# Expert stage: both rows of a pair are added up by the matrix engine alone, without quarter sums on POOL

## Chip, cores and metric

One core of one Trainium2 chip. The metric is the device time of the kernel in microseconds (us), median of several runs. Engines are named as in the profile: PE is TensorE's matmul, PEld its weight load, DVE is VectorE, ACT is ScalarE, POOL is GpSimd, SP is SyncE, whose queue carries the DMAs.

## What is computed

A block of four layers on x of shape (1, 128, 128, 32) in float32; each layer is a token mixer and a channel mixer, both with a residual. The change touches the last channel mixer alone, a mixture of 8 experts with the best 2 per token:

```
router_probs = softmax(x @ router_w + router_b)
top_p, top_i = top_k(router_probs, 2);  top_p = top_p / sum(top_p)
expert_out = einsum('bnd,edc->bnec', x, expert_w) + expert_b
out = einsum('bnk,bnkc->bnc', top_p, take_along_axis(expert_out, top_i[..., None], axis=2))
t = t + out
```

The kernel multiplies all 8 expert outputs of a token by its weights (zero for the 6 that were not chosen) and adds the 8 products up.

## The kernel before

The kernel is written engine by engine: each engine has its own list of instructions in program order, and semaphores hold them together. The eight layer parts follow one another (t0, f0, t1, r1, the scan, r2, t3, f3 in the blocks from L1972 on). The change touches f3, the expert stage, which is the last.

In f3 the 128 x 128 tokens lie as 32 steps s (S = 32) of 128 partitions with G = 4 groups each, so a step has 4 x 32 = 128 output columns (GC) for each of 8 experts: 1024 products a partition. Two steps make a pair j; there are 16 pairs (EPAIRS). The work on a pair goes round four engines:

- PE, expert(s), L1760: the product of the normalised tokens with all expert weights, 4 matmuls of 256 columns into four PSUM banks (L1772, even s; each uses 32 rows of the array) or two banks (L1767, odd s; 64 rows). It waits until the weighing of step s - 2 has read the bank (semaphore e_mul).
- DVE, weigh(s), L1867: one operation over 128 x 1024 that multiplies the products in PSUM by the token's weights and writes WEIGHED in SBUF (L1871).
- POOL, half_sum(s), L1907: adds experts 4 to 7 to experts 0 to 3, 128 x 512, into HALVES (L1909). HALVES has four slots of pairs; a slot holds [expert quarter e = 0..3][step of the pair][128 columns].
- POOL, quarter_sum(j), L1912: for the odd step of the pair alone, adds quarters 2 and 3 to 0 and 1 in place, 128 x 256 (L1914). It follows the odd step's half sum and waits for it (e_half).
- PE, add_up(j), L1775: adds what is left with matmuls against the identity, which sum in PSUM: quarter 0 of both steps (256 columns, L1787), quarters 2 and 3 of the even step alone (128 columns each, L1789), quarter 1 of both steps (256 columns, L1790).
- DVE, add_pair(j), L1874: adds x from SBUF to the sum in PSUM and writes x_rows (L1876); SP stores four rows at a time from there.

The order on PE is expert(2j), expert(2j + 1), add_up(j - 2) (SUM_LAG = 2); on DVE weigh(2j), weigh(2j + 1), add_pair(j - 2). DVE also does the routing of the second half of the tokens between the weighings of pairs 1 to 5 (L1881 to L1888; L1833, L1834 and L1853 are among it). The half sum of the last step, 31, and the quarter sum of the last pair run on DVE (L1893 to L1895), with a semaphore of their own (e_last).

A float32 matmul is two weight loads and two matmul instructions in the trace, so that one call of pe.matmul shows as "x2".

Of the kernel before, what the change touches and what calls it, by code (L numbers as in the profile page):

```python
# [28 lines left out]
GC = G * C  # L29
# [9 lines left out]
E3 = 8  # L39
# [75 lines left out]
def build(nc, x_d, par_d, row_d, mask_d, w1_d, w2_d, w2l_d, out_d):  # L115
    with ExitStack() as ctx:
        def sb(name, shape, dt=F32):
            return ctx.enter_context(nc.sbuf_tensor(name, shape, dt))

        def sem(name):  # L120
            return ctx.enter_context(nc.semaphore(name))
# [3 lines left out]
        XC = sb("x_cols", [N, NC])  # L125
# [13 lines left out]
        ident = sb("ident", [N, N])  # L139
# [11 lines left out]
        eps = sb("eps", [N, 4])  # L151
# [8 lines left out]
        last = sb("last", [C, G, C])  # L160
# [5 lines left out]
        def bank(b, cols=BANK, n=1):  # L166
            return PSUM[:, b * BANK:b * BANK + (n - 1) * BANK + cols]
# [42 lines left out]
        def stage(name, kinds, own="", src=None, dst=None, scratch=None, eps=0, e2=0.0):  # L210
            L = Stage(name, src, dst, scratch, eps, e2)
            for kind in kinds.split():
                if kind not in shared:
                    shared[kind] = [0, {}]
                    for word in families[kind].split():
                        shared[kind][1][word.split(":")[0]] = sem(f"{kind}_{word.split(':')[0]}")
                before, sems = shared[kind]
                shared[kind][0] += 1
                for word in families[kind].split():
                    key, n = word.split(":")  # L220
                    L.s[key], L.at[key] = sems[key], before * int(n)
            for key in own.split():
                L.s[key], L.at[key] = sem(f"{name}_{key}"), 0
            return L
# [15 lines left out]
        def wait_all(eng, levels):  # L240
            for s, v in levels:
                eng.wait_ge(s, v)
# [9 lines left out]
        v2 = stage("V2", "turn_x")  # L252
        r2 = stage("R2", "scale last turn rec check", "g_ps g_y0 g_y1 g_edge_ps g_edge g_turned y_ps done", src=XC, eps=1, e2=0.0)
        t3 = stage("L3", "norm last weights ones tri", src=XC, scratch=XR, eps=0, e2=EPS)
        f3 = stage("F3", "norm last ones turn", "c_dve w_dve w_pe rank hot rt_ps top diff sg e_ps e_mul e_half e_last e_quart e_sum done", src=XC, eps=1, e2=0.0)


        x_done = lambda L: [(L.s["done"], L.at["done"] + S // 4)]
# [203 lines left out]
        def turn_z_pe(pe, L, b):  # L462
            wait_z(pe, L, b)
            if "one" in L.s:
                pe.wait_ge(L.s["one"], L.at["one"] + b + 1)
            if b >= 2:
                pe.wait_ge(L.s["zt"], L.at["zt"] + b - 1)
            for k in range(4):
                m = pe.transpose(bank(b % 2)[:, k * N:(k + 1) * N], block_of(Z)(4 * b + k), ident[:, :])  # L469
            m.then_inc(L.s["zt_ps"], 1)  # L470
# [414 lines left out]
        top = sb("top", [N, 6, K0])  # L885
# [808 lines left out]
        rank = sb("rank", [N, E3], BF16)  # L1694
# [6 lines left out]
        EPAIRS = S // 2  # L1701
        SUM_LAG = 2
        WEIGHED = GATE[:, :].rearrange("p (k f) -> p k f", k=4)
        HALVES = Z[:, :].rearrange("p (j e k f) -> p j e k f", j=4, e=E3 // 2, k=2)
# [30 lines left out]
        def f3_pe(pe):  # L1735
            L = f3
            pe.wait_ge(L.s["w_dve"], L.at["w_dve"] + 2)

            def route(b):

                pe.wait_ge(L.s["zt"], L.at["zt"] + b + 1)
                for s in range(4 * b, 4 * b + 4):
                    m = pe.matmul(bank(6 + s // 16)[:, s % 16 * G * E3:(s % 16 + 1) * G * E3], ZT[:, s, :], wr[:, :, :],
                                  start=True, stop=True)
                return m

            for b in range(S // 4):
                turn_z_pe(pe, L, b)
                if b == 3:
                    wait_all(pe, L.early_banks_free)  # L1750
                    for a in range(b - 1):
                        route(a)
                if b >= 3:
                    m = route(b - 1)
                if b == 4:
                    m.then_inc(L.s["rt_ps"], 1)
            wait_all(pe, L.banks_free)
            route(7).then_inc(L.s["rt_ps"], 1)

            def expert(s):  # L1760
                if s >= 2:
                    pe.wait_ge(L.s["e_mul"], L.at["e_mul"] + s - 1)
                if s % 2:
                    for q in range(2):
                        for h in range(2):
                            rows = slice(h * HALF_ROWS, (h + 1) * HALF_ROWS)
                            m = pe.matmul(bank(4 + h)[:, q * E3 * C:(q + 1) * E3 * C], ZT[rows, s, :], we[rows, q, :],  # L1767
                                          start=True, stop=True)
                else:
                    for g in range(G):  # L1770
                        rows = slice(g * C, (g + 1) * C)
                        m = pe.matmul(bank(g, E3 * C), ZT[rows, s, :], we[rows, g % 2, :], start=True, stop=True)  # L1772
                m.then_inc(L.s["e_ps"], 1)

            def add_up(j):  # L1775

                pe.wait_ge(L.s["e_half"], L.at["e_half"] + min(2 * j + 2, S - 1))
                if j < EPAIRS - 1:
                    pe.wait_ge(L.s["e_quart"], L.at["e_quart"] + j + 1)
                else:  # L1780
                    pe.wait_ge(L.s["e_last"], L.at["e_last"] + 2)
                if j == 0:
                    pe.wait_ge(L.s["top"], L.at["top"] + F3_LOGITS_READ)
                if j >= 2:
                    pe.wait_ge(L.s["done"], L.at["done"] + j - 1)
                o = bank(6 + j % 2, 2 * GC)
                pe.matmul(o, ident[:, :], HALVES[:, j % 4, 0, :, :], start=True, stop=False)  # L1787
                for e in (2, 3):
                    pe.matmul(o[:, 0:GC], ident[:, :], HALVES[:, j % 4, e, 0, :], start=False, stop=False)  # L1789
                pe.matmul(o, ident[:, :], HALVES[:, j % 4, 1, :, :], start=False, stop=True).then_inc(L.s["e_sum"], 1)  # L1790

            for j in range(EPAIRS):
                expert(2 * j)
                expert(2 * j + 1)
                if j >= SUM_LAG:
                    add_up(j - SUM_LAG)
            for j in range(EPAIRS - SUM_LAG, EPAIRS):
                add_up(j)
# [10 lines left out]
        def f3_dve(dve):  # L1809
            L = f3  # L1810
# [80 lines left out]
                    add_pair(j - SUM_LAG)  # L1891
            dve.wait_ge(L.s["e_mul"], L.at["e_mul"] + S)
            half_sum(dve, S - 1, "e_last")  # L1893
            dve.wait_ge(L.s["e_last"], L.at["e_last"] + 1)
            quarter_sum(dve, EPAIRS - 1, "e_last")  # L1895
            for j in range(EPAIRS - SUM_LAG, EPAIRS):
                add_pair(j)

# [8 lines left out]
        def half_sum(eng, s, done="e_half"):  # L1907
            halves = WEIGHED[:, s % 4, :].rearrange("p (a e f) -> p a e f", a=2, f=GC)
            eng.tensor_tensor(HALVES[:, s // 2 % 4, :, s % 2, :], halves[:, 0], halves[:, 1], ALU.add)\  # L1909
                .then_inc(f3.s[done], 1)  # L1910

        def quarter_sum(eng, j, done="e_quart"):  # L1912
            halves = HALVES[:, j % 4, :, 1, :]
            eng.tensor_tensor(halves[:, 0:2], halves[:, 0:2], halves[:, 2:4], ALU.add).then_inc(f3.s[done], 1)  # L1914

        def f3_pool(pool):
            L = f3
            for a in range(2):
                half = slice(a * N // 2, (a + 1) * N // 2)
                pool.wait_ge(L.s["sg"], L.at["sg"] + 2 * a + 1)  # L1920
                pool.tensor_tensor(RT[5][:, half], RT[1][:, half], W1S[:, half].unsqueeze(2).to_broadcast([N, N // 2, E3]),
                                   ALU.mult).then_inc(L.s["hot"], 1)
            for s in range(S - 1):
                pool.wait_ge(L.s["e_mul"], L.at["e_mul"] + s + 1)
                if s >= 8:
                    pool.wait_ge(L.s["e_sum"], L.at["e_sum"] + s // 2 - 3)
                half_sum(pool, s)
                if s % 2:
                    pool.wait_ge(L.s["e_half"], L.at["e_half"] + s + 1)
                    quarter_sum(pool, s // 2)  # L1930


        for L, b, col in ((t0, 2, 0), (t1, 0, 0), (t3, 1, 0), (f3, 4, 0), (r1, 5, 0), (r2, 5, GC)):
# [165 lines left out]
```

## Time and profile before

| | |
|---|---|
| runs | 531.54, 531.96, 533.02 us (median 531.96) |
| profiled execution | 531.37 us, span 529.5 us |
| busy | PE 425.5 us (80%), DVE 366.6 (69%), ACT 234.5 (44%), POOL 227.2 (43%) |
| mean granted TensorE clock | 0.900 of full speed (2.4 GHz) |
| expert stage | from about 461 us to the end |

The span goes from the first to the last instruction; the run's time has some 2 us more around it. A share of busy time is a mean over all layers, most of which the change does not touch; for the change it is the expert stage that has to be read. PE's rows are pipelined: the row of a matmul includes the way through the array, so that rows of one engine overlap, and the start of one row to the start of the next tells what an instruction costs in a sequence. Where several instructions of a line follow one another, the timeline shows them as one row with their count.

### The profile page before, as it was taken

What the parts mean: (1) busy time and instruction counts of PE and PEld (TensorE: products, weight loads), DVE (VectorE), ACT (ScalarE), POOL (GpSimd) and SP (SyncE); (2) the same over time, 40 slices, a digit from 0 to 9 for tenths busy, and PEclk for the clock granted to TensorE, in tenths of its full rate; (3) what the DMA queues carried; (4) which work ended last, traced back from release to release, by engine and by line L of the source; (5) the groups of instructions that cost most, each with busy time, mean ns of one, the idle gap of its engine ahead of it and who ended that gap; (6) DMA issues with size and microseconds to landing.
All of it is one profiled execution on the core that took longest, in us unless ns stands there. A gap on an engine that the chain in (4) does not pass through costs nothing.

```text
span 529.5 us, 8983 instructions
## 1 busy us (share of the span) xinstructions
PE 425.5 (80%) x3226; PEld 321.7 (61%) x3226; DVE 366.6 (69%) x1191; ACT 234.5 (44%) x577; POOL 227.2 (43%) x294
## 2 busy tenths in 40 slices
PE   2788866987698866998599968698589877869995
PEld 2455853566344853797399945598355866736664
DVE  4887688748798388637634467301979389998885
ACT  1397654621577456677400038476369553300000
POOL 2499178001477078000000035000349369268994
PEclk9999999778799899999779979799579978569999
DMA  9400000000000000000000000000000000001223
GB/s 170 84 2 1 1 1 0 1 3 0 1 2 1 0 2 1 1 2 1 2 0 1 1 3 0 1 2 1 0 2 2 1 0 1 2 0 20 41 45 56
DMA packets 34671, 6.05 MB, mean 11 GB/s; under 512 B 33713, under 2 KB 34369, under 8 KB 34626
## 3 DMA queue, kind: packets, MB, share of 16 engines
q1 hardware_dynamic: 34626, 5.46, 5.9%
q8 instruction: 27, 0.44, 0.3%
q14 instruction: 18, 0.15, 0.1%
HBM read 3.36 MB, written 2.10 MB: 10 GB/s over the span
## 4 chain that ended last, share of the span: by engine, by line
PE 48%; DVE 37%; ACT 5%; POOL 5%; issue 3%; DMA 1%; SPq 1%; DVEq 0%; POOLq 0%
PE psum L1594 7%; DVE ab L750 6%; PE psum L1167 5%; DVE moments L334 5%; PE psum L1166 5%; DVE ab L734 5%; PE psum L469 3%; PE psum L624 3%; PE psum L1767 3%; POOL z L394 2%; PE psum L594 2%; PE psum L635 2%; PE psum L1787 2%; POOL gate L812 2%; PE psum L1772 2%
## 5 line engine op out<-in xcount | busy, mean ns | idle before, releaser
L594 PE MATMUL psum<-wp_L,z_t 64*128 64x320 f32 x384 | 66.1, 473 | 3.4 <-ACT z_t L372 2.1
L334 DVE BATCH_NORM_STATS2 moments<-x_cols 128x6 f32<-128x64 f32 x448 | 61.8, 214 | 3.1 <-ACT x_cols L873 1.8
L469 PE MATMUL psum<-ident,z 128*128 128x128 f32 x224 | 43.4, 332 | 22.3 <-POOL z L394 19.4
L469 PEld LDWEIGHTS psum<-ident,z 128*128 128x128 f32 x224 | 31.2, 170 | 45.7 <-POOL z L394 33.1
L372 ACT ACTIVATE z_t<-psum 128x512 f32<-128x512 f32 x56 | 40.0, 720 | 31.1 <-PE psum L469 30.9
L594 PEld LDWEIGHTS psum<-wp_L,z_t 64*128 64x128 f32 x384 | 33.3, 192 | 31.0 <-issue 27.6
L389 POOL MEMSET z<- 128x16 f32 x32 | 4.0, 126 | 112.1 <-DVE z L320 111.7
L1302 ACT ACTIVATE ab<-psum,mv 128x128 f32<-128x128 f32 x108 | 39.7, 368 | 16.2 <-PE psum L1167 5.9
L1167 PE MATMUL psum<-ab,R_vt 128*128 128x128 f32 x216 | 45.7, 294 | 0.0
L812 POOL TENSOR_TENSOR gate<-gate,stats 128x512 f32<-128x512 f32 x24 | 25.2, 1050 | 44.2 <-DVE stats L775 43.9
L1166 PE MATMUL psum<-z_t,wbnt 128*128 128x128 f32 x216 | 43.3, 283 | 0.8 <-DVE wbnt L1364 0.8
L635 PE MATMUL psum<-wo_L,z_t 64*128 64x128 f32 x384 | 29.8, 297 | 15.7 <-DVE x_cols L783 8.5
L1594 PE MATMUL psum<-ab,toep 128*128 128x128 f32 x324 | 39.0, 284 | 4.1 <-POOL ab L1575 3.1
L1594 PEld LDWEIGHTS psum<-ab,toep 128*128 128x128 f32 x324 | 38.7, 199 | 4.5 <-issue 4.5
L1909 POOL TENSOR_TENSOR z<-gate 128x512 f32<-128x512 f32 x31 | 39.9, 1304 | 1.4 <-DVE gate L1871 1.4
L1871 DVE TENSOR_TENSOR gate<-psum,ab 128x1024 f32<-128x1024 f32 x32 | 37.9, 1220 | 3.1 <-PE psum L1772 3.0
L362 ACT ACTIVATE stats<-moments,eps 128x16 f32<-128x16 f32 x56 | 17.3, 309 | 48.6 <-DVE moments L334 48.5
L750 DVE TENSOR_TENSOR ab<-psum,sig 128x256 f32<-128x256 f32 x64 | 34.6, 608 | 6.0 <-ACT sig L681 6.0
L635 PEld LDWEIGHTS psum<-wo_L,z_t 64*128 64x128 f32 x384 | 25.4, 199 | 20.7 <-ACT z_t L702 10.7
L681 ACT ACTIVATE sig<-psum 128x256 f32<-128x256 f32 x96 | 36.8, 384 | 0.0
L718 POOL TENSOR_TENSOR x_rows<-gate,bo_L 128x512 f32<-128x512 f32 x24 | 30.6, 1276 | 12.4 <-ACT gate L677 12.3
L1166 PEld LDWEIGHTS psum<-z_t,wbnt 128*128 128x128 f32 x216 | 34.0, 198 | 1.3 <-DVE wbnt L1364 1.3
(271 smaller groups left out, 905.3 us busy)
## 6 DMA issues: line engine op xcount, KB each, us to landing
x_cols<-in_x_dram SPq DMA_DIRECT2D x16, 128.0 KB, 2.8
out_dram<-x_rows SPq DMA_DIRECT2D x32, 64.0 KB, 1.9
par<-in_par_dram SPq DMA_DIRECT2D x1, 644.5 KB
w<-in_w_dram SPq DMA_DIRECT2D x4, 64.0 KB, 2.3
w<-in_w_dram SPq DMA_DIRECT2D x1, 256.0 KB, 2.5
mask<-in_mask_dram SPq DMA_DIRECT2D x1, 64.0 KB, 2.8
row<-in_row_dram SPq DMA_DIRECT2D x1, 3.3 KB
w_bias<-in_w_dram SPq DMA_DIRECT2D x1, 8.0 KB, 1.8
```

Source lines behind the costliest of these rows:

```text
L334: m = dve.bn_stats(moments[:, q, k:k + 2, :].rearrange("p k m -> p (k m)"), X4[:, SQ * q + s, g:g + 2, :].rearrange("p g c -> p c g"))
L372: act.activation(dst, bank(q % 2).rearrange("p (s n) -> p s n", s=4), ACT.Copy).then_inc(L.s["zt"], 1)
L469: m = pe.transpose(bank(b % 2)[:, k * N:(k + 1) * N], block_of(Z)(4 * b + k), ident[:, :])
L594: m = pe.matmul(bank(slot_bank(s) + h, 2 * 5 * C), ZT[rows, s, :], wp[l][rows, :, :], start=True, stop=True)
L635: m = pe.matmul(o_bank(b)[:, :, 2 * h:2 * h + 2, k, :], ZT[rows, 4 * b + k, :], wo[l][rows, :, rows].rearrange("p w (g c) -> p w g c", g=2 ...
L750: dve.tensor_tensor(to_ab(s).rearrange("p (h g) w -> p h g w", h=2), slot(s)[:, :, :, 2 * C:4 * C], sig, ALU.mult).then_inc(L.s["lin"], 1)
L1166: return (pe.matmul(o, W["wbnt"][:, :], chunks(ZTIME, off, h), start=True, stop=False), lambda: pe.matmul(o, W["vt"][:, :], chunks(Y, off, ...
L1167: lambda: pe.matmul(o, W["vt"][:, :], chunks(Y, off, h), start=False, stop=True))
L1302: act.activation(chunks(Y, first + k + 1, h), bank(2 * h + (before + k) % 2, NS), ACT.Sigmoid, bias=bias).then_inc(L.s[f"step_y{h}"], 1)
L1594: m = pe.matmul(bank(2 + h, ROWS_S * NB), toep[:, b, :, :], scan_rows(SCN[:, :, b:b + NB], off, h), start=(b == 0), stop=(b == 2))
L1871: dve.tensor_tensor(WEIGHED[:, s % 4, :].rearrange("p (e g c) -> p e g c", e=E3, g=G), f3_out(s), wts[:, s].unsqueeze(3).to_broadcast([N, ...
L1909: eng.tensor_tensor(HALVES[:, s // 2 % 4, :, s % 2, :], halves[:, 0], halves[:, 1], ALU.add)\
```

## The change

The quarter sums are gone on POOL and on DVE, with their semaphore e_quart. add_up(j) takes all four quarters of both steps: four matmuls of 256 columns against the identity, in one accumulation. It waits for the half sums (e_half), and in the last pair for one event of e_last instead of two.

```diff
@@ add_up(j), PE
                 pe.wait_ge(L.s["e_half"], L.at["e_half"] + min(2 * j + 2, S - 1))
-                if j < EPAIRS - 1:
-                    pe.wait_ge(L.s["e_quart"], L.at["e_quart"] + j + 1)
-                else:
-                    pe.wait_ge(L.s["e_last"], L.at["e_last"] + 2)
+                if j == EPAIRS - 1:
+                    pe.wait_ge(L.s["e_last"], L.at["e_last"] + 1)
...
                 o = bank(6 + j % 2, 2 * GC)
-                pe.matmul(o, ident[:, :], HALVES[:, j % 4, 0, :, :], start=True, stop=False)
-                for e in (2, 3):
-                    pe.matmul(o[:, 0:GC], ident[:, :], HALVES[:, j % 4, e, 0, :], start=False, stop=False)
-                pe.matmul(o, ident[:, :], HALVES[:, j % 4, 1, :, :], start=False, stop=True).then_inc(L.s["e_sum"], 1)
+                for e in range(E3 // 2):
+                    m = pe.matmul(o, ident[:, :], HALVES[:, j % 4, e, :, :], start=(e == 0), stop=(e == E3 // 2 - 1))
+                m.then_inc(L.s["e_sum"], 1)
@@ f3_dve, after the last weighing
             half_sum(dve, S - 1, "e_last")
-            dve.wait_ge(L.s["e_last"], L.at["e_last"] + 1)
-            quarter_sum(dve, EPAIRS - 1, "e_last")
@@ quarter_sum
-        def quarter_sum(eng, j, done="e_quart"):
-            halves = HALVES[:, j % 4, :, 1, :]
-            eng.tensor_tensor(halves[:, 0:2], halves[:, 0:2], halves[:, 2:4], ALU.add).then_inc(f3.s[done], 1)
@@ f3_pool
                 half_sum(pool, s)
-                if s % 2:
-                    pool.wait_ge(L.s["e_half"], L.at["e_half"] + s + 1)
-                    quarter_sum(pool, s // 2)
```

The end of PE's list shows the last expert products and the add_ups of pairs 13 to 15. A row's count is of calls of pe.matmul; the semaphores that it waits for stand behind it (names begin with the stage, F3). Before:

```order
L1772 MATMUL psum<-we,z_t 128x256 [waits F3_e_mul]
L1772 MATMUL psum<-we,z_t 128x256 x3
L1767 MATMUL psum<-we,z_t 128x256 [waits F3_e_mul]
L1767 MATMUL psum<-we,z_t 128x256 x3
L1787 MATMUL psum<-z,ident 128x256 [waits F3_done,F3_e_quart,F3_e_half]
L1789 MATMUL psum<-z,ident 128x128 x2
L1790 MATMUL psum<-z,ident 128x256
```

With the change:

```order
L1772 MATMUL psum<-we,z_t 128x256 [waits F3_e_mul]
L1772 MATMUL psum<-we,z_t 128x256 x3
L1767 MATMUL psum<-we,z_t 128x256 [waits F3_e_mul]
L1767 MATMUL psum<-we,z_t 128x256 x3
L1786 MATMUL psum<-z,ident 128x256 [waits F3_done,F3_e_half]
L1786 MATMUL psum<-z,ident 128x256 x3
```

The place of add_up in the list is the same; it is four matmuls as before, two of them twice as wide, and one wait fewer at its head.

The end of DVE's list, from the last weighing on. Before:

```order
L1871 TENSOR_TENSOR gate<-psum,ab 128x1024 x2
L1876 TENSOR_TENSOR x_rows<-x_cols,psum 128x2x4x32
L1909 TENSOR_TENSOR z<-gate 128x4x128
L1914 TENSOR_TENSOR z<-z 128x2x128
L1876 TENSOR_TENSOR x_rows<-x_cols,psum 128x2x4x32 x2
```

With the change:

```order
L1868 TENSOR_TENSOR gate<-psum,ab 128x1024 x2
L1873 TENSOR_TENSOR x_rows<-x_cols,psum 128x2x4x32
L1904 TENSOR_TENSOR z<-gate 128x4x128
L1873 TENSOR_TENSOR x_rows<-x_cols,psum 128x2x4x32 x2
```

The quarter sum between the last half sum and the last two adds to x is gone (line numbers are smaller by 3 to 5). On POOL the fifteen quarter sums are gone from between the half sums, and the 31 half sums follow one another.

## Rows read from the trace of the kernel before

**Rows 1.** The chain of waits, 450 us to the end, shares by line (longest first).
```profile
by line: PE psum L1767 18.7%; PE psum L1787 12.5%; PE psum L1772 11.3%; PE psum L1789 8.8%; PE psum L1790 8.5%; DVE gate L1871 7.4%; issue 4.0%; DVE ranks L1833 3.4%; DVE ab L1839 2.8%; DVE ranks L1834 2.7%; DVE rmax L1838 2.6%; DVE ab L185
```

**Rows 2.** Busy time by stretch: us, busy us (instructions) by engine, granted clock, DMA.
```profile
487.00:521.00 34.00, 33.97 (x252) 22.37 (x248) 29.99 (x33) 0.00 (x0) 33.14 (x32) 1.00 0.25 40
```

**Rows 3.** Timeline of one pair: start us, us, engine, line, operation, idle before and releaser.
```profile
511.36 0.71 PE L1772 MATMUL psum<-we,z_t 32*128 32x256 f32 x8
...
511.54 2.50 POOL L1909 TENSOR_TENSOR z<-gate 128x512 f32<-128x512 f32 x2
...
512.01 1.13 PE L1767 MATMUL psum<-we,z_t 64*128 64x256 f32 x8
512.14 2.36 DVE L1871 TENSOR_TENSOR gate<-psum,ab 128x1024 f32<-128x1024 f32 x2 [0.25 <-PE psum L1772]
513.07 0.30 PEld L1787 LDWEIGHTS psum<-z,ident 128*128 128x128 f32 x2 [0.33 <-POOL z L1909]
513.07 0.70 PE L1787 MATMUL psum<-z,ident 128*128 128x256 f32 x2
...
513.61 0.61 PE L1789 MATMUL psum<-z,ident 128*128 128x128 f32 x4
...
514.05 0.60 PE L1790 MATMUL psum<-z,ident 128*128 128x256 f32 x2
514.12 0.73 POOL L1914 TENSOR_TENSOR z<-z 128x256 f32<-128x256 f32 x1
...
514.58 0.71 PE L1772 MATMUL psum<-we,z_t 32*128 32x256 f32 x8
```

**Rows 4.** Line L1790 from 487 to 521 us: duration in ns, min/median/max.
```profile
L1790 PE MATMUL psum<-z,ident x22: 379/380/382, 488.2 to 520.7; 128*128 128x256 f32 x22
```

**Rows 5.** Timeline of PE around the first add_up, 470 to 484 us.
```profile
474.22 2.08 PE L1767 MATMUL psum<-we,z_t 64*128 64x256 f32 x8 [1.02 <-DVE gate L1871]
476.23 1.22 PE L1787 MATMUL psum<-z,ident 128*128 128x256 f32 x2
477.24 1.06 PE L1789 MATMUL psum<-z,ident 128*128 128x128 f32 x4
478.10 0.91 PE L1790 MATMUL psum<-z,ident 128*128 128x256 f32 x2
478.93 0.71 PE L1772 MATMUL psum<-we,z_t 32*128 32x256 f32 x8
```

**Rows 6.** Busy time by stretch, where the granted clock rises.
```profile
478.00:479.00 1.00, 1.00 (x8) 0.50 (x7) 0.12 (x1) 0.00 (x0) 0.80 (x1) 0.64 0.00 0
```

**Rows 7.** Timeline from 452 us, routing operations of DVE.
```profile
464.04 0.42 DVE L1834 TENSOR_TENSOR ranks<-ranks,rank 128x512 bf16<-128x512 bf16 x1
...
472.07 0.83 DVE L1834 TENSOR_TENSOR ranks<-ranks,rank 128x512 bf16<-128x512 bf16 x1
...
484.07 0.79 DVE L1853 TENSOR_TENSOR ab<-ab,squares 128x512 f32<-128x512 f32 x1
```

**Rows 8.** Timeline of the end of the stage, from 517.5 us.
```profile
517.79 0.71 PE L1772 MATMUL psum<-we,z_t 32*128 32x256 f32 x8
...
518.06 2.50 POOL L1909 TENSOR_TENSOR z<-gate 128x512 f32<-128x512 f32 x2
...
521.31 1.27 POOL L1909 TENSOR_TENSOR z<-gate 128x512 f32<-128x512 f32 x1
...
521.46 0.67 PE L1787 MATMUL psum<-z,ident 128*128 128x256 f32 x2 [0.37 <-issue]
521.46 1.67 DVE L1909 TENSOR_TENSOR z<-gate 128x512 f32<-128x512 f32 x1
...
523.16 0.42 DVE L1914 TENSOR_TENSOR z<-z 128x256 f32<-128x256 f32 x1
...
523.68 0.67 PE L1787 MATMUL psum<-z,ident 128*128 128x256 f32 x2 [0.68 <-issue]
...
525.27 0.42 DVE L1876 TENSOR_TENSOR x_rows<-x_cols,psum 128x256 f32<-128x256 f32 x1 [1.36 <-PE psum L1790]
```

More of the change, by code:

```diff
@@ L254, in build @@
         t3 = stage("L3", "norm last weights ones tri", src=XC, scratch=XR, eps=0, e2=EPS)
-        f3 = stage("F3", "norm last ones turn", "c_dve w_dve w_pe rank hot rt_ps top diff sg e_ps e_mul e_half e_last e_quart e_sum done", src=XC, eps=1, e2=0.0)
+        f3 = stage("F3", "norm last ones turn", "c_dve w_dve w_pe rank hot rt_ps top diff sg e_ps e_mul e_half e_last e_sum done", src=XC, eps=1, e2=0.0)
         x_done = lambda L: [(L.s["done"], L.at["done"] + S // 4)]
```

## Prediction

> **What bounds the kernel now.** I read the chain of waits first, cut to the last 80 us [rows 1]: nearly all of the change's stage is a chain of matrix engine (PE) lines, the two expert products (L1767, L1772) and the four matmuls of add_up (L1787 to L1790); the weighing on VectorE (L1871) holds 7.4%, and no POOL line is among the large shares. Then the busy time by stretch [rows 2]: from 487 to 521 us PE is busy 33.97 of 34.00 us at a granted clock of 1.00, POOL 33.14, DVE 29.99. Two engines look full, so the timeline of one pair of rows has to tell which sets the pace [rows 3]. PE goes round from one even expert product to the next in 514.58 - 511.36 = 3.22 us, and each of its lines starts where the one before gives way: 0.65 for the even product, 1.06 for the odd one, 0.54 + 0.44 + 0.53 = 1.51 for add_up. POOL needs 3.26 (its halves start at 511.54 [rows 3] and, two pairs on, at 518.06 [rows 8]), so it falls behind by 0.04 a pair. Yet PE does not wait for it: pair 12's quarter sum is there at 514.12 + 0.73 = 514.85 us, and its add_up comes a round after pair 11's, at 513.07 + 3.22 = 516.29 [rows 3]. Only pair 14's, with no expert product ahead of it, finds POOL late: the two half sums before it end at 518.06 + 2.50 = 520.56, its quarter sum some 0.8 later, and the add_up, ready 1.71 + 1.51 after pair 15's product at 521.01, starts at 521.46 [rows 8]. So PE sets the pace, POOL is 1% behind the bound, DVE has 0.44 us a pair to spare (2.36 + 0.42 of 3.22).
>
> The row that could mislead is the weight load's "0.33 idle, POOL z L1909" [rows 3]. The same 0.33 stands before other groups with other releasers, and the half sum that it names had ended long before; I read it as the fixed cost of a group's head, not as a wait for POOL.
>
> **What the change does to PE, pair by pair.** An identity matmul over 128 columns becomes one over 256, twice in each of 16 pairs; each is two instructions in the trace. L1789's four instructions take 514.05 - 513.61 = 0.44 us, 0.11 each [rows 3]. For 256 columns the spacing follows from L1790: two instructions span 0.60 us and the second lasts 0.38 [rows 4], so it starts 0.22 after the first. Four instructions go from 0.11 to 0.22: **+0.44 us a pair**, and the pace becomes 3.22 + 0.44 = 3.66. Bounds: nothing, if the head's 0.33 were room; and 2 x 0.53 - 0.44 = +0.62, if every new matmul cost what a whole L1787 or L1790 takes from its start to the next line's (0.54, 0.53), which has a group's head or a change of line in it. The new ones lie in the middle of a group, as L1787's second instruction does, so I take 0.44.
>
> From pair 3's even product (478.93 us [rows 5]) to pair 15's (517.79 [rows 8]) are 12 rounds in 38.86 us. Twelve at 3.216 would be 38.59; the remaining 0.27 comes from two extra routing operations on DVE in pairs 4 and 5 (the first is the 0.79 of L1853 [rows 7]). At 3.66 DVE's 2.78 + 0.79 = 3.57 fits in a round, so these no longer show. 12 x 0.44 - 0.27 = **+5.0 us**.
>
> **The first add_up** lies in the low clock: its two L1789 matmuls take 478.10 - 477.24 = 0.86 [rows 5], and the granted clock is 0.64 between 478 and 479 us, where it goes from the 1.2 GHz level to the 2.4 GHz level [rows 6]. PE had been busy without a break since 474.22. If the clock rises at the same moment (about 478.7), 1.4 of the 1.72 us that four wide instructions of 0.43 take are spent when it rises, the rest goes at half the price: +0.6 instead of +0.87, or +0.44 if it rose earlier. I take **+0.6**.
>
> **What leaves POOL and DVE.** Fifteen quarter sums leave POOL (0.73 each in the steady part, of which none but the last is on the path). With them POOL's round is 2.50 in 3.66, and its half sums come earlier than now; nothing else waits for it. The cover of this saving is PE: as long as PE needs over 2.50, POOL's gain is worth nothing. Only at the end does it count. The matmuls also lose a wait on the semaphore of the quarter sums; what is queued behind is on PE itself.
>
> **The end**, counted from pair 15's even product (T = 517.79) [rows 8]. Now: add_up of pair 13 at T + 1.71, of 14 at + 3.67 (after POOL's late quarter sum), DVE's half sum of row 31 from 521.46 for 1.67 us (it ends 0.55 after POOL's half sum of row 30, started at 521.31, of usual length 1.27), its quarter sum 0.42, then the last add_up at 523.68 and the last add to x at 525.27, T + 7.48. Changed: add_up of 13 is 1.95 long, so 14 starts at + 3.66 and 15 at + 5.61. By then both half sums are there: POOL's at about + 3.3 without the lag, DVE's from + 4.1 for 0.6 to 1.7. The last add_up takes 525.27 - 523.68 = 1.59 + 0.44, so the last add to x stands at + 7.64: **+0.2 us**. What POOL and DVE save here (some 1.1 us) is what three longer add_ups give back. The stores behind it are the same. Bounds -0.3 and +0.4, for the 0.42 of the quarter sum and its wait either way.
>
> One price stays open at the start. DVE's routing work of row 471 to 473 is on the path, and L1834 takes 0.83 there against 0.42 where POOL is idle [rows 7]. POOL will run the next half sum there instead of the quarter sum. I take 0, between -0.5 (no overlap) and +0.5 (one more such collision).
>
> **Sum:** 5.0 + 0.6 + 0.2 = +5.8 us. The profiled execution had 531.37 us, which makes 537.2; it lies 0.59 below the median of the runs (531.96), on which the same sum gives 537.8. I give 537.5. With the bounds (-0.2 and +0.3 for the first add_up, -0.3 and +0.4 for the end, 0.5 each way for the start, and the runs' own 531.54 to 533.02) the forecast's own range is 535.7 to 539.2.
>
> **Rivals.**
>
> (a) *The pace stays, the new columns fit into the 0.33 us before each group.* For it: those gaps are in the rows as idle time of the weight load. Against it: PE's matmul rows leave 0.03 us of 34 open [rows 2], and starts follow column counts (0.11 for 128, 0.22 for 256). Then only the end changes: add_up of 14 at + 3.22, of 15 at + 4.73, the last add at + 6.3, so -1.1 us: 530.3, inside no change. Chance 0.05.
>
> (b) *Faster: POOL sets the pace.* POOL's round (3.26) is longer than PE's (3.22), and PE's rows stretch by waiting inside it. The quarter sums gone, the next bound is DVE's 2.78: 12 x 0.44 = 5.3 us less, with the 1.1 at the end 525.0. It decides in its favour if PE's true work in a pair, with the 0.44 added, is under 2.78. For it: POOL is busy 33.14 of 34 and named as the releaser of L1787. Against it: the 1.44 us between pair 12's quarter sum and its add_up, and the spacing by columns. Chance 0.03.
> The Trainium skill ("Perfetto Trace Analysis", Identifying the Most-Contended Engine) says that matmul busy time is no good measure of TensorE's headroom, and to take the busy share of the weight loads instead. By that rule PE would be 22.37 / 34 = 66% used here, with 1.1 us of a pair free: this rival's case. I hold the starts of the rows against it.
>
> (c) *Slower than forecast: each new matmul at the upper price.* 0.62 a pair: 12 x 0.62 - 0.27 = 7.2, with 0.8 for the first and 0.4 for the end 8.4 us: 539.8 on the profiled execution, 540.4 on the median. Chance 0.07.
>
> (d) *The clock rises one pair later.* At the low level the odd product takes 2.01 us from start to start (474.22 to 476.23 [rows 5]) against 1.06, so a pair that is still at that level costs some 3.2 us more: 540.7. PE's activity before the rise is the same as now, which speaks against it. Chance 0.05.
>
> **How the numbers follow.** The forecast has 0.80. A difference of 0.3% (1.6 us) is about what a measurement of this kernel tells from none; slower by more are the forecast, (c) and (d): 0.92; within it is (a): 0.05; faster is (b): 0.03. The range of 535.7 to 539.2 is that of the forecast and leaves out the four rivals, 0.20 together.
>
> **What would show it.** In the changed profile: 64 add_up matmuls of 256 columns, 128 instructions; the pair's round at 3.65 to 3.66 us at granted clock 1.00; PE without gaps from about 474 us; POOL idle over 1 us in each round, waiting for DVE's weighing; DVE idle about 0.9 a round, waiting for PE; the last two add_ups starting back to back. A round under 3.4 us would refute the price of a column or the claim that PE is full; a round over 3.8 the spacing in the group; a round of 3.66 with a sum far from +5.8 us would put the error into the first add_up or the end.

## The result and the profile after

The changed kernel took 539.16 us in the median (536.87 to 542.87, 4 runs) beside 532.1 of the kernel before: a ratio of 1.014 (95% interval 1.0102 to 1.0179). The direction was forecast, the size was not: on the median of 531.96 the ratio gives 539.4 us, above the forecast of 537.5 and just above its range. Measured twice more the ratio was 1.0116 (1.0084 to 1.0148) and 1.0103 (1.007 to 1.0136). Over all runs, which come from more than one chip, the medians are 537.99 us (16 runs) and 531.66 (81 runs of the kernel before): **6.3 us** is the better estimate of what the change costs.

The profiled execution of the changed kernel had 540.68 us and a span of 538.7. Its steady part is what the prediction said. One round of a pair (timeline; columns as in [rows 3]):

```profile
519.98 0.71 PE L1772 MATMUL psum<-we,z_t 32*128 32x256 f32 x8
...
521.69 1.99 PE L1786 MATMUL psum<-z,ident 128*128 128x256 f32 x8
522.07 2.50 POOL L1904 TENSOR_TENSOR z<-gate 128x512 f32<-128x512 f32 x2 [1.14 <-DVE gate L1868]
...
523.61 0.71 PE L1772 MATMUL psum<-we,z_t 32*128 32x256 f32 x8
523.72 0.42 DVE L1873 TENSOR_TENSOR x_rows<-x_cols,psum 128x256 f32<-128x256 f32 x1 [0.60 <-PE psum L1786]
```

523.61 - 519.98 = 3.63 us against 3.22 [rows 3]. Add_up now goes from 521.69 to 523.61, 1.92 us instead of 1.51. POOL runs two half sums and then waits 1.14 us a round for the weighing, DVE waits 0.60 for add_up. The busy time by stretch, in the row that answers to [rows 2]:

```profile
487.00:521.00 34.00, 34.00 (x230) 22.61 (x230) 26.84 (x31) 0.00 (x0) 24.51 (x20) 1.00 0.25 40
```

PE is full as before (34.00 of 34), at the same granted clock; POOL has gone from 33.14 to 24.51. In the chain of waits from 450 us on, the line that does all of add_up stands first with 35.3%, where its three parts had 29.8% together [rows 1]:

```profile
by line: PE psum L1786 35.3%; PE psum L1767 17.0%; PE psum L1772 10.7%; DVE gate L1868 4.0%; DVE ranks L1830 3.0%; DVE ranks L1831 3.0%; DVE ab L1836 2.5%; issue 2.4%; DVE moments L334 2.4%; DVE rmax L1835 2.3%; DVE ab L1843 1.6%; DVE squar
```

The end of the stage (timeline, answering to [rows 8]) has no wait for POOL left:

```profile
527.25 0.71 PE L1772 MATMUL psum<-we,z_t 32*128 32x256 f32 x8
...
528.95 5.45 PE L1786 MATMUL psum<-z,ident 128*128 128x256 f32 x24
529.33 1.27 POOL L1904 TENSOR_TENSOR z<-gate 128x512 f32<-128x512 f32 x1 [1.13 <-DVE gate L1868]
530.99 0.42 DVE L1873 TENSOR_TENSOR x_rows<-x_cols,psum 128x256 f32<-128x256 f32 x1 [0.60 <-PE psum L1786]
...
532.71 0.42 DVE L1873 TENSOR_TENSOR x_rows<-x_cols,psum 128x256 f32<-128x256 f32 x1 [0.70 <-PE psum L1786]
534.44 0.42 DVE L1873 TENSOR_TENSOR x_rows<-x_cols,psum 128x256 f32<-128x256 f32 x1 [1.31 <-PE psum L1786]
```

Three add_ups run back to back (528.95, 24 instructions); the adds to x follow at 1.72 us, and the last is 534.44 - 527.25 = 7.19 us behind pair 15's even product, against 7.48.

The opening is where the profile differs from the forecast:

```profile
473.27 4.16 POOL L1904 TENSOR_TENSOR z<-gate 128x512 f32<-128x512 f32 x3
...
476.24 0.72 PE L1772 MATMUL psum<-we,z_t 32*128 32x256 f32 x8
476.34 1.37 DVE L1831 TENSOR_TENSOR ranks<-ranks,rank 128x512 bf16<-128x512 bf16 x1
...
479.02 1.44 PE L1767 MATMUL psum<-we,z_t 64*128 64x256 f32 x8 [2.06 <-DVE gate L1868]
...
480.39 3.33 PE L1786 MATMUL psum<-z,ident 128*128 128x256 f32 x8
...
483.65 0.71 PE L1772 MATMUL psum<-we,z_t 32*128 32x256 f32 x8
```

DVE's second routing operation of pair 1 (L1831, before: L1834) takes 1.37 us instead of 0.83 [rows 7]. PE then stands idle for 2.06 us ahead of the odd product of pair 2, and the first add_up takes 483.65 - 480.39 = 3.26 us, where the steady part needs 1.92. It runs at the 1.2 GHz level almost throughout, as the busy time by stretch shows (columns as in [rows 6]; the clock is the third number from the end):

```profile
480.00:482.00 2.00, 2.00 (x8) 1.34 (x5) 1.97 (x3) 0.00 (x0) 1.54 (x2) 0.50 0.00 0
```

This profile also began the stage late: pair 0's even product is at 466.07 us, against 461.81 before. No instruction ahead of that was changed. The first products of all fourteen profiles of this study, most of changed stages, lie between 459.39 and 466.07, of the kernel before at 461.81 and 463.70, of the changed one at 466.07, 461.76 and 461.94: the layers ahead end earlier or later from execution to execution, and this one drew the latest. That is 4.3 of the 9.2 us between the two profiled spans, and it is no part of the change.

### The profile page after: what moved, and what is told of

Same layout as the page of the kernel before. It is cut to its first block, busy times and chain, and to the rows that moved or that the text cites. A ratio compares the mean times of both kernels' runs of the same rounds, so it can differ in the third digit from the quotient of the medians.

```text
span 538.7 us, 8966 instructions
## 1 busy us (share of the span) xinstructions
PE 435.9 (81%) x3226; PEld 330.7 (61%) x3226; DVE 366.2 (68%) x1190; ACT 234.2 (43%) x577; POOL 216.0 (40%) x279
## 2 busy tenths in 40 slices
DMA packets 34670, 6.04 MB, mean 11 GB/s; under 512 B 33713, under 2 KB 34369, under 8 KB 34626
## 4 chain that ended last, share of the span: by engine, by line
PE 51%; DVE 35%; ACT 5%; POOL 4%; issue 3%; DMA 1%; SPq 1%; DVEq 0%; POOLq 0%
PE psum L1594 7%; DVE ab L750 6%; PE psum L1786 6%; DVE moments L334 5%; PE psum L1167 5%; PE psum L1166 5%; DVE ab L734 5%; PE psum L469 3%; PE psum L624 3%; PE psum L1767 3%; PE psum L635 2%; PE psum L594 2%; POOL z L394 2%; PE psum L1772 2%; ACT z_t L372 2%
```

## The experiments

The stage is cut in three parts below, all start to start: the opening from the even product of pair 0 to that of pair 3, twelve rounds from there to pair 15, the end from there to the last add to x. (Some expectations count the opening from the last routing matmul, which is 0.3 to 0.4 us more.)

| kernel | opening | 12 rounds | end | stage |
|---|---|---|---|---|
| before, two profiles | 17.12, 14.99 | 38.86, 39.76 | 7.48, 7.45 | 63.46, 62.20 |
| changed, three profiles | 17.58, 17.84, 17.58 | 43.60, 43.59, 43.59 | 7.19 | 68.37, 68.62, 68.36 |
| changed, quarter sums left on POOL | 15.41, 15.41 | 43.92, 43.91 | 7.19 | 66.52, 66.51 |
| changed, pair 0's quarter sum left | 15.42 | 44.34 | 7.19 | 66.95 |
| changed, half sum of row 2 held | 15.01, 14.99 | 44.36, 44.36 | 7.19 | 66.56, 66.54 |
| half the change | 14.93 | 41.48 | 6.78 | 63.19 |
| before without quarter sums | 17.04 | 38.81 | 6.04 | 61.89 |
| before, held | 14.59 | 39.96 | 7.47 | 62.02 |
| before, held, two pairs wide | 14.59 | 39.96 | 6.78 | 61.33 |

When PE begins its idle time ahead of the odd product of pair 2, the granted clock is at 1.00 in twelve of these fourteen profiles (early rise). In the first of the kernel before and the second of the changed kernel it is 0.50 there and rises within the first add_up (late rise; 0.64 and 0.65 from 478 to 479 us). These two are compared with one another, the others among themselves.

### The changed kernel once more

No edit.

> The changed kernel once more, to see how its 7.1 us over the kernel before divide. Theory A (columns on PE, and in the layers ahead a granted clock that falls out anew in every execution): the round of a pair is 3.63 us again, the expert stage is 4.9 us longer than before (from the last routing matmul to the last add to x), and whatever is over that lies ahead of the stage, where the times of the runs spread over some 6 us, at mean clocks from 0.886 to 0.900; runs of the kernel before spread likewise when there are more of them. Theory B (the change itself slows the layers ahead): every run of this kernel has its stage begin 2 to 6 us later than the kernel before, and the runs of the kernel before stay within 1.5 us. Median by A 536.5 to 538.5 or what the draw gives, by B 539 again.

Measured: ratio 1.0116 (1.0084 to 1.0148), median 538.26 of 6 runs. The round is 3.63 again. In this profile the stage began at 461.76, as before (461.81), and the clock rose at the same point of the stage, so it can be laid on the first profile of before: 68.62 - 63.46 = 5.2 us longer, +0.7 in the opening, +4.7 in the rounds, -0.3 at the end. The first add_up and the idle time ahead of it (timeline), and the clock by stretch:

```profile
474.71 2.08 PE L1767 MATMUL psum<-we,z_t 64*128 64x256 f32 x8 [1.56 <-DVE gate L1868]
...
476.72 2.95 PE L1786 MATMUL psum<-z,ident 128*128 128x256 f32 x8
...
479.60 0.71 PE L1772 MATMUL psum<-we,z_t 32*128 32x256 f32 x8
```

```profile
476.00:478.00 2.00, 2.00 (x7) 1.17 (x6) 1.93 (x3) 0.00 (x0) 1.22 (x1) 0.50 0.00 0
```

Theory B does not hold: its profile begins no later, and 26 runs of the kernel before on that chip reach from 529.27 to 535.42. But theory A leaves over a microsecond of the 6.3 unexplained.

### Only PE widened: quarter sums stay on POOL

```diff
+        QSCR = sb("qscr", [N, 2, GC])
...
                 half_sum(pool, s)
+                if s % 2:
+                    pool.wait_ge(L.s["e_half"], L.at["e_half"] + s + 1)
+                    halves = HALVES[:, s // 2 % 4, :, 1, :]
+                    pool.tensor_tensor(QSCR[:, :, :], halves[:, 0:2], halves[:, 2:4], ALU.add)
```

Nobody reads QSCR.

> The changed kernel with the fifteen quarter sums left on POOL, written to a buffer that nobody reads, so that PE's four wide matmuls and their waits stay as changed. Theory A: PE's round stays 3.63 us since POOL's 3.26 fits into it; the stage is as long as the changed one to 0.4 us (only the last half sum on POOL could be later). Rival (POOL's freed time is worth something): the stage is longer than the changed one by up to 15 x 0.04 = 0.6 us in the rounds or by 0.7 at the end.

Measured: 1.0068 (1.0038 to 1.0097), median 535.69; measured again 1.0061 (1.0037 to 1.0085), 535.99. One round in the first profile:

```profile
511.45 0.71 PE L1773 MATMUL psum<-we,z_t 32*128 32x256 f32 x8
...
512.48 0.72 POOL L1923 TENSOR_TENSOR qscr<-z 128x256 f32<-128x256 f32 x1
...
515.08 0.71 PE L1773 MATMUL psum<-we,z_t 32*128 32x256 f32 x8
```

The round is 3.63 us with the quarter sum (L1923) in it, and the end is the same 7.19: in the steady part POOL's freed time is worth nothing, as predicted. Yet with more work the kernel is faster by some 2 us than the changed one (535.88 and 537.99 over all runs), which neither theory had. The table shows where: in the opening, 15.41 against 17.6 to 17.8.

### Only POOL relieved: no quarter sums, narrow matmuls

```diff
-                if j < EPAIRS - 1:
-                    pe.wait_ge(L.s["e_quart"], L.at["e_quart"] + j + 1)
-                else:
-                    pe.wait_ge(L.s["e_last"], L.at["e_last"] + 2)
+                if j == EPAIRS - 1:
+                    pe.wait_ge(L.s["e_last"], L.at["e_last"] + 1)
...
-            dve.wait_ge(L.s["e_last"], L.at["e_last"] + 1)
-            quarter_sum(dve, EPAIRS - 1, "e_last")
...
-                if s % 2:
-                    pool.wait_ge(L.s["e_half"], L.at["e_half"] + s + 1)
-                    quarter_sum(pool, s // 2)
```

This kernel leaves quarters 2 and 3 of the odd steps out of the sum.

> The kernel before without any quarter sum and without the wait for it, PE's four matmuls as narrow as before; quarters 2 and 3 of the odd steps are left out of the sum. Theory A (PE sets the pace): the round stays 3.22 us, only the end gains, about 1.1 us: 530.3 to 531. Rival (POOL sets the pace): the round falls to DVE's 2.8 to 3.0, 4 to 6 us less: 525 to 528.

Measured: 0.9987 (0.996 to 1.0015), median 530.67. A round in its profile:

```profile
512.74 0.71 PE L1772 MATMUL psum<-we,z_t 32*128 32x256 f32 x8
...
514.45 0.30 PEld L1785 LDWEIGHTS psum<-z,ident 128*128 128x128 f32 x2 [0.33 <-POOL z L1905]
...
514.83 2.50 POOL L1905 TENSOR_TENSOR z<-gate 128x512 f32<-128x512 f32 x2 [0.72 <-DVE gate L1869]
...
515.96 0.71 PE L1772 MATMUL psum<-we,z_t 32*128 32x256 f32 x8
```

515.96 - 512.74 = 3.22 us, unchanged, with POOL idle for 0.72 of it (the timeline's wait for the weighing). The rival in which POOL sets the pace falls. The weight load of the first add_up matmul (L1785) has its "0.33 idle, POOL" here too, with POOL far ahead: it is the fixed price of a group's head. The end gains 1.4 us (6.04). The opening does not gain: L1832 (L1834 before) takes 1.37 us here as well, against 0.83 [rows 7].

```profile
473.60 1.37 DVE L1832 TENSOR_TENSOR ranks<-ranks,rank 128x512 bf16<-128x512 bf16 x1
...
476.28 1.29 PE L1767 MATMUL psum<-we,z_t 64*128 64x256 f32 x8 [1.99 <-DVE gate L1869]
```

```profile
478.00:480.00 2.00, 2.00 (x8) 1.52 (x7) 1.97 (x2) 0.00 (x0) 0.79 (x1) 0.50 0.00 0
```

PE is idle for 1.99 us ahead of the odd product of pair 2, and the granted clock, 1.00 from 474 to 476 us, is 0.50 from 478 to 480. So the opening is 17.04 us here against 14.99 in the second profile of before, without one wide matmul.

### Half the change

```diff
-                for e in (2, 3):
-                    pe.matmul(o[:, 0:GC], ident[:, :], HALVES[:, j % 4, e, 0, :], start=False, stop=False)
+                pe.matmul(o, ident[:, :], HALVES[:, j % 4, 2, :, :], start=False, stop=False)
+                pe.matmul(o[:, 0:GC], ident[:, :], HALVES[:, j % 4, 3, 0, :], start=False, stop=False)
...
-            eng.tensor_tensor(halves[:, 0:2], halves[:, 0:2], halves[:, 2:4], ALU.add).then_inc(f3.s[done], 1)
+            eng.tensor_tensor(halves[:, 1], halves[:, 1], halves[:, 3], ALU.add).then_inc(f3.s[done], 1)
```

> Half the change: quarter 2 goes to PE with both steps (256 columns), quarter 3 keeps its quarter sum on POOL (128 x 128, into quarter 1) and its 128 columns on PE. Theory A: the round is 3.216 + 0.21 = 3.42 us, the stage 12 x 0.21 - 0.27 + 0.3 = some 2.5 us longer than before, half of what the change costs. Rival (a fixed price of the wider form, or one of the waits): the round is that of the kernel before or of the changed one, 3.22 or 3.63.

Measured: 1.0023 (0.9998 to 1.0048), median 532.2. One round:

```profile
511.30 0.71 PE L1772 MATMUL psum<-we,z_t 32*128 32x256 f32 x8
...
513.55 0.59 PE L1788 MATMUL psum<-z,ident 128*128 128x256 f32 x2
...
513.98 0.38 PE L1789 MATMUL psum<-z,ident 128*128 128x128 f32 x2
...
514.20 0.60 PE L1790 MATMUL psum<-z,ident 128*128 128x256 f32 x2
...
514.73 0.71 PE L1772 MATMUL psum<-we,z_t 32*128 32x256 f32 x8
```

The wide matmul (L1788) takes 0.43 us from start to start, the narrow one (L1789) 0.22: the price of a column is confirmed, the round is 3.43 us. The total was overestimated: +1.0 us in the stage, 0.23% in the times, instead of 2.5. Against the second profile of before, whose clock rose as early, the rounds cost only 41.48 - 39.76 = 1.7 us, since the routing operations on DVE, which stretch twelve rounds of the fast kernel to 39.76 us where 12 x 3.216 would be 38.59, fit better into the longer ones, and the end gains 0.7.

### What the opening hides: a hold on POOL

Theory C was formed on the openings above: with the quarter sum of pair 0 gone, POOL's half sums of rows 1 and 2 follow one another, and DVE's routing operation finds the second in its way.

```diff
             for s in range(S - 1):
...
+                if s == 2:
+                    pool.wait_ge(L.s["top"], L.at["top"] + 22)
                 half_sum(pool, s)
```

> The changed kernel, with POOL's half sum of row 2 held until DVE's second routing operation of pair 1 (line L1831) is done, so that the two no longer collide. Theory C (at the opening of the stage POOL's half sums of rows 1 and 2 now follow one another and keep DVE's L1831 waiting: 1.37 us against 0.83, which delays the third weighing, leaves PE idle longer ahead of the odd product of pair 2, and with that keeps PE at 1.2 GHz for the first add_up in more executions): L1831 takes 0.42, PE's idle time there falls from 1.6 or 2.1 us to under 1.2, the opening (last routing matmul to even product of pair 3) from 18.0 to 17.2 or, with the clock up, to 15.5; median 535 to 537 against 538.3 of the changed kernel. Theory A alone (columns, and a clock drawn anew each time): 0 to 0.9 us less, no more.

Measured: 1.0067 (1.0042 to 1.0092), median 536.32; L1831 takes 0.42, the opening is 15.01. For a comparison on one chip the changed kernel, the held one, the one with its quarter sums and the kernel before were run side by side:

> The changed kernel a third time, now on one chip beside the three that differ from it in one point each. Theory C (a collision of POOL and DVE at the opening, and through PE's longer gap a low clock at the first add_up): L1831 takes 1.37 us, the first add_up is at least partly at 1.2 GHz (opening 17.5 to 17.8 us), and the median lies 1.5 to 3 us over that of the same kernel with the hold. Theory A: no more than 0.9 us over it.

> The changed kernel with POOL's half sum of row 2 held until DVE's routing operation is done, on the same chip. Theory C: opening 15.0 us, median 1.5 to 3 us under the changed kernel and some 4 over the kernel before. Theory A: within 0.9 of the changed kernel.

> The changed kernel with all quarter sums left on POOL, unread, on the same chip. Theory C: as the hold to 0.5 us. Theory A: as the changed kernel to 0.5 us.

> The kernel before under a name of its own, for a second profile and as a measure of what two runs of the same program differ by: ratio 1.000 with an interval of some 0.3% each way. The opening is 17.0 us if the clock rises late as in the first profile, or 15 if it rises ahead of the first add_up; the stage's 12 rounds 38.9 us where they run at 2.4 GHz.

Measured: changed 537.44 us, 1.0103 (1.007 to 1.0136); held 536.31, 1.0077 (1.0049 to 1.0105); with quarter sums 535.99, 1.0061 (1.0037 to 1.0085); before 0.9982 (0.9957 to 1.0007). The medians of this chip differ by 1.1 and 1.45 us, less than theory C asked for and more than A allowed; over all runs they are 537.99 (16 runs), 536.32 (12) and 535.88 (20). The profiles decide it, since in these two the stages began at the same time (461.94 and 461.96 us). The changed kernel, timeline of the opening:

```profile
469.14 4.16 POOL L1904 TENSOR_TENSOR z<-gate 128x512 f32<-128x512 f32 x3
...
472.21 1.37 DVE L1831 TENSOR_TENSOR ranks<-ranks,rank 128x512 bf16<-128x512 bf16 x1
...
474.89 1.44 PE L1767 MATMUL psum<-we,z_t 64*128 64x256 f32 x8 [2.07 <-DVE gate L1868]
...
476.26 3.33 PE L1786 MATMUL psum<-z,ident 128*128 128x256 f32 x8
...
479.52 0.71 PE L1772 MATMUL psum<-we,z_t 32*128 32x256 f32 x8
```

and by stretch:

```profile
472.00:474.00 2.00, 0.82 (x10) 0.32 (x8) 1.93 (x3) 0.00 (x0) 1.29 (x1) 0.96 0.00 0
...
476.00:478.00 2.00, 2.00 (x6) 1.47 (x5) 1.93 (x3) 0.00 (x0) 1.41 (x2) 0.50 0.00 0
```

The held one, in the same two views:

```profile
469.15 2.49 POOL L1904 TENSOR_TENSOR z<-gate 128x512 f32<-128x512 f32 x2
...
472.22 0.42 DVE L1831 TENSOR_TENSOR ranks<-ranks,rank 128x512 bf16<-128x512 bf16 x1
...
472.79 3.71 POOL L1904 TENSOR_TENSOR z<-gate 128x512 f32<-128x512 f32 x3 [1.15 <-DVE ranks L1831]
...
473.96 1.13 PE L1767 MATMUL psum<-we,z_t 64*128 64x256 f32 x8 [1.13 <-DVE gate L1868]
...
475.02 2.00 PE L1786 MATMUL psum<-z,ident 128*128 128x256 f32 x8
...
476.95 0.71 PE L1772 MATMUL psum<-we,z_t 32*128 32x256 f32 x8
```

```profile
472.00:474.00 2.00, 0.87 (x12) 0.36 (x10) 1.93 (x4) 0.00 (x0) 1.21 (x1) 0.97 0.00 0
474.00:476.00 2.00, 2.00 (x13) 1.52 (x14) 1.97 (x3) 0.00 (x0) 2.00 (x3) 1.00 0.00 0
476.00:478.00 2.00, 1.66 (x13) 0.87 (x11) 1.97 (x2) 0.00 (x0) 0.50 (x1) 1.00 0.00 0
```

In both the clock rises at the same point (0.96 and 0.97 from 472 to 474). With POOL's third half sum directly behind the second (4.16 us in one piece, to 473.30), L1831 ends at 473.58, PE waits 2.07 us, and from 476 to 478 us the clock is back at 0.50, so that the first add_up takes 3.26 us (476.26 to 479.52). With the hold POOL starts it at 472.79, PE waits 1.13 us, the clock stays at 1.00, and the first add_up takes 1.93 (475.02 to 476.95, where the even product of pair 3 starts). The Trainium skill ("SBUF — State Buffer", section "SBUF: two separate sides") says that a GpSimd operation and a VectorE operation with two SBUF inputs take a shared port pair in turn, each for its whole length; the trace agrees, L1831 ending 0.28 us after POOL's half sum, where it needs 0.42 by itself.

The hold does not keep all that it gains. DVE's next operation of this kind, L1836, takes 1.39 us beside a half sum of POOL (L1839 in the kernel before: 0.94), PE waits 0.70 us for the weighing ahead of pair 3's odd product, and that round is 4.41 us instead of 3.63.

### One quarter sum left

```diff
+        QSCR = sb("qscr", [N, 2, GC])
...
                 half_sum(pool, s)
+                if s == 1:
+                    pool.wait_ge(L.s["e_half"], L.at["e_half"] + s + 1)
+                    halves = HALVES[:, s // 2 % 4, :, 1, :]
+                    pool.tensor_tensor(QSCR[:, :, :], halves[:, 0:2], halves[:, 2:4], ALU.add)
```

> The changed kernel with one quarter sum left on POOL, that of pair 0, written to a buffer that nobody reads. Theory C: that one operation was what kept the half sum of row 2 away from DVE's routing work; L1831 is 0.83 again, and the median falls to that of the kernel with all fifteen left (535.7). Theory A: it stays at 538 to 538.5.

Measured: 1.0075 (1.0043 to 1.0108), median 536.34, runs from 532.36 to 539.98. The opening is 15.42 and the routing operation takes 0.83, as theory C has it, but the runs spread so far that the median alone would settle nothing.

### The kernel before with the hold, and with a wide end

The same hold stands one step earlier, ahead of pair 0's quarter sum; the second kernel also gives the last two pairs four wide matmuls and no quarter sum. The two added POOL lines are the hold and stand in both; all else is in the second alone.

```diff
-                if j < EPAIRS - 1:
+                if j < EPAIRS - 2:
...
+                    if j < EPAIRS - 2:
+                        pe.matmul(o[:, 0:GC], ident[:, :], HALVES[:, j % 4, e, 0, :], start=False, stop=False)
+                    else:
+                        pe.matmul(o, ident[:, :], HALVES[:, j % 4, e, :, :], start=False, stop=False)
...
-            quarter_sum(dve, EPAIRS - 1, "e_last")
...
                 half_sum(pool, s)
+                if s == 1:
+                    pool.wait_ge(L.s["top"], L.at["top"] + 22)
...
-                if s % 2:
+                if s % 2 and s < S - 4:
```

> The kernel before with the same hold, ahead of the quarter sum of pair 0: L1834 falls from 0.83 to 0.42 and L1833 perhaps to 0.69, the third weighing starts 0.4 to 0.5 us sooner. Theory C: 0.4 us less where the clock rises late, up to 2.5 where it now rises ahead of the first add_up; median 529 to 531 against 531.2. Theory A: 0 to 0.5 less.

> The same, and the last two pairs alone with four wide matmuls and no quarter sum, since only the end of the stage waits for them: from the even product of pair 15 to the last add to x 6.9 us instead of 7.48. Median 0.5 us under that of the kernel with the hold alone.

Measured: 0.9994 (0.9968 to 1.0019) and 0.9975 (0.9944 to 1.0006), medians 531.66 and 530.79, with the kernel before at 532.22 beside them; the hold alone was expected at 529 to 531. The hold brings the opening to 14.59, 0.4 less than the second profile of before, of which the rounds give 0.2 back to DVE; the wide end saves 0.7 (6.78 against 7.45). The second kernel is the fastest form found that computes the whole sum, by 0.9 us in the stage (61.33 against 62.20), and its ratio is not clear of 1.

## Why the prediction was right or wrong

**PE sets the pace, POOL's time is free: right.** The round stayed 3.22 us with POOL relieved and 3.63 with POOL as loaded as before. Rivals (a) and (b) are refuted, and with (b) the reading by weight loads: these were busy 22.61 of 34 us after the change, 66% as before, on an engine without room.

**+0.44 us a pair: right to 0.03.** The round grew by 3.63 - 3.22 = 0.41 to 0.42 us; a wide matmul inside a group takes 0.43, where rival (c) needs 0.53. Twelve rounds were put at +5.0 and were +4.7 against the first profile, where the forecast's account of the clock holds.

**The end, +0.2: too high by 0.5.** It was -0.29. I gave the add_ups of pairs 13 and 14 the 1.95 us that one takes between two expert products, and the last a head of its own; back to back they follow at 1.72, without the head of a group between them.

**The opening: wrong, and with it the size.** The step that failed is "I take 0, between -0.5 (no overlap) and +0.5 (one more such collision)", with the sentence before it that POOL will run the next half sum in the quarter sum's place. It does, and the half sum is longer: L1834 went from 0.83 to 1.37 us, the upper bound, in all three profiles of the changed kernel. I then treated this as a price of half a microsecond, and left the clock out of it: the first add_up was to find "the clock rises at the same moment", and against (d) I held that PE's activity before the rise was the same. It was not. The collision lengthens PE's idle time ahead of the odd product of pair 2 by some 0.53 us: from 1.02 to 1.56 in the profiles with the late rise, from 1.54 to 2.07 in those with the early one. In the first and third profile of the changed kernel the clock was up ahead of this gap, fell back behind it and reached the 2.4 GHz level again only during the first add_up. In the second it had not risen yet, as in the first profile of before. Rival (d) in its own form did not occur: pair 3's even product takes 0.71 us in all three.

With the collision taken away the stage of the early rise is 66.55 us instead of 68.37: **1.8 us**, of which the opening has 2.6 and the rounds give 0.8 back. With the quarter sums left on POOL and unread it is 66.52, and with that of pair 0 alone 66.95, so the hold is not the only way to that. The runs' medians point the same way, with 1.1 us side by side and 1.7 over all runs (537.99 - 536.32).

So, early rise against early rise, the change costs 6.2 us (68.37 - 62.20): some 4.4 us of columns and end (66.55 - 62.20) and 1.8 us of the collision with its clock. The first profile of before, on which I worked, has a late rise, so that a fall of the clock cannot show against it: there the change costs 5.2 us (68.62 - 63.46), and 5.8 was 0.6 too high, 0.3 in the rounds and 0.5 at the end, while the opening came out at +0.7 for a forecast of +0.6, though made up otherwise: 0.5 of the collision (474.71 instead of 474.22 [rows 5] for pair 2's odd product) and 0.2 of the first add_up. That the opening comes close there is luck. I had taken the clock of one execution for that of the kernel.

**Two sums of the prediction do not come out.** The +0.6 for the first add_up leaves out that L1790 would follow at the full clock: four wide instructions from 477.24, with the clock rising at 478.7, would end at 478.83, and L1790 would then take 0.53 us instead of 0.83, which makes 479.36 instead of 478.93, or +0.4 (an estimate from [rows 3] and [rows 5]). And the bounds given for the range, 1.0 down and 1.2 up, with the runs' own 0.42 and 1.06, reach from 536.1 to 539.8 around 537.5, not from 535.7 to 539.2.

**What stays open.** The clock rose late in one profile of two of the kernel before and in one of three of the changed one. What makes it late is not shown, and how often each kernel meets it can't be counted from times alone, so the shares of the 6.3 us over all runs are not known as closely as those of the profiles. The first four runs' 7.1 us, against 6.3 over all, I put down to the starts of the stage; only one of those four has a profile.

## What to carry over

An operation that is off the critical path may still be what keeps two other operations apart. Before removing it, look at what its engine does next in the same place, and whether that takes a shared port from the engine on the path at the one spot where this one has no slack. Where an engine is full in its own order, price added work by start-to-start spacing inside a group, and check the ramp of the stage separately, where the granted clock still moves.

## What was not expected

A gap of PE's bears on the clock at a finer grain than I had thought. After 2.07 us idle (changed kernel, third profile) the granted clock, 0.96 from 472 to 474 us, was 0.50 from 476 to 478, in the next add_up; after 1.54 us it stayed up, in the second profile of the kernel before (timeline):

```profile
473.97 0.83 DVE L1834 TENSOR_TENSOR ranks<-ranks,rank 128x512 bf16<-128x512 bf16 x1
...
476.12 1.13 PE L1767 MATMUL psum<-we,z_t 64*128 64x256 f32 x8 [1.54 <-DVE gate L1871]
...
478.69 0.71 PE L1772 MATMUL psum<-we,z_t 32*128 32x256 f32 x8
```

There the granted clock is 1.00 in every stretch from 474 to 480 us, and the first add_up is over by 478.69. All twelve profiles with the early rise part in this way: the clock fell in the three with a gap of 1.99, 2.06 and 2.07 us and stayed up in the nine with 1.04 to 1.54. No run has a gap in between.

And a gain at the opening is not kept: with the early rise the twelve rounds of the kernel before take 39.76 us instead of 38.86, because DVE, whose routing operations lie in pairs 1 to 5, then sets the start of some (PE waits 0.67 us for the weighing in pair 3).
